# Graph network kernel, one core: a different order of ScalarE's copies and TensorE's matmuls at the turn from one batch of edges to the next

## What is computed

```
edge_index = jnp.stack([src, dst])
x = _layernorm(x + _L0_gnn_ref(x, src, dst), axis=-1)          # mean of the neighbours
x = _layernorm(x + _L1_gnn_ref(x, edge_weight, edge_attr_3, edge_index, w1, b1, w2, b2), axis=-1)
```

## Time and profile before

| | us |
|---|---|
| median of 3 runs | 3803.33 |
| lowest and highest | 3798.77, 3803.84 |
| the profiled execution | 3798.03 |
| its span, first to last instruction | 3796.3 |

### The profile page before, as it was taken

The page is one execution under the profiler, slowest core; times in us unless marked ns, Lnnn a source line. Parts: engine busy times, 40 slices in busy tenths (PEclk is TensorE's granted clock), DMA queues, the critical chain, the costliest instruction groups (busy, mean ns, idle before and its releaser), DMA issues.

```text
span 3796.3 us, 58108 instructions
## 1 busy us (share of the span) xinstructions
PE 3310.6 (87%) x17312; PEld 1902.1 (50%) x17312; DVE 2762.8 (73%) x3470; ACT 2061.5 (54%) x2391; POOL 2786.3 (73%) x2915
## 2 busy tenths in 40 slices
PE   4999999999999883399999999999999999999963
PEld 3898889898989783222323232333323232323232
DVE  5787877787878785467777777777777777777765
ACT  4777777776777660145454545454554545454520
POOL 6777777777777776677777777777777777777746
PEclk9999999999999995599999999999999999999975
DMA  4122222222122211122222222222222222222211
GB/s 100 39 57 41 52 43 43 50 44 54 40 55 43 50 48 29 39 57 53 62 55 59 55 59 55 59 58 56 62 52 62 55 59 54 59 55 59 57 28 26
DMA packets 188428, 197.65 MB, mean 52 GB/s; under 512 B 60241, under 2 KB 149427, under 8 KB 188085
## 3 DMA queue, kind: packets, MB, share of 16 engines
q1 hardware_dynamic: 95508, 149.13, 13.7%
q0 software_dynamic: 92832, 47.72, 9.7%
HBM read 134.02 MB, written 62.59 MB: 52 GB/s over the span
## 4 chain that ended last, share of the span: by engine, by line
PE 70%; ACT 12%; DVE 5%; POOL 5%; issue 5%; DMA 1%; SPq 0%; ACTq 0%; DVEq 0%; POOLq 0%
PE ps_r L940 19%; PE ps_r L990 17%; PE ps_m L1027 10%; PE ps_m L940 10%; PE ps_r L1018 8%; ACT prod_room L822 8%; POOL ngot L667 4%; DVE unit L1645 3%; PE ps_m L1037 2%; PE ps_r L1002 2%; ACT f_across L829 2%; PE ps_r L924 1%; ACT hot_s L739 1%; PE ps_m L1043 1%; ACT hot_s L742 1%
## 5 line engine op out<-in xcount | busy, mean ns | idle before, releaser
L688 POOL DMA_INDIRECT got<-x_d,idx x1564 | 1506.2, 963 | 530.6 <-issue 504.7
L822 ACT ACTIVATE prod_room<-ps_r,bias_col 128x1024 f32<-128x1024 f32 x392 | 435.9, 1112 | 780.0 <-PE ps_r L990 531.9
L940 PE MATMUL ps_r<-x_hi,hot_s 128*128 128x448 f32 x1974 | 741.6, 376 | 41.7 <-ACT hot_s L742 41.7
L1645 DVE TENSOR_TENSOR x_room<-radial_more,ps_r 128x1024 f32<-128x1024 f32 x392 | 475.0, 1212 | 384.0 <-PE ps_r L1018 252.3
L990 PE MATMUL ps_r<-hid,wc 64*128 64x512 f32 (+1 forms) x2352 | 669.8, 646 | 81.2 <-ACT prod_room L822 72.9
L940 PE MATMUL ps_r<-x_lo,hot_s 128*128 128x448 f32 x1974 | 733.0, 371 | 0.0
L739 ACT ACTIVATE hot_s<-rows,minus_row 128x512 fp32r<-128x512 f16 (+1 forms) x658 | 449.0, 764 | 244.0 <-PE ps_m L940 206.2
L1018 PE MATMUL ps_r<-ft,repeat 32*128 32x512 f32 (+1 forms) x2352 | 553.4, 639 | 1.1 <-ACT ft L848 0.6
L1645 DVE TENSOR_TENSOR unit<-prod_room,ps_r 128x1024 f32<-128x1024 f32 x392 | 451.1, 1213 | 106.9 <-PE ps_r L1018 102.0
L940 PEld LDWEIGHTS ps_r<-x_hi,hot_s 128*128 128x128 f32 x1974 | 378.3, 192 | 75.5 <-issue 43.0
L990 PEld LDWEIGHTS ps_r<-hid,wc 64*128 64x128 f32 x2352 | 178.8, 186 | 448.8 <-ACT prod_room L822 255.3
(11 more groups left out here) (203 smaller groups left out, 4438.4 us busy)
## 6 DMA issues: line engine op xcount, KB each, us to landing
hid<-weight_t SPq DMA_DIRECT2D x196, 256.0 KB
run_d<-runs_t SPq DMA_DIRECT2D x194, 256.0 KB
got<-x_d,idx POOLq DMA_INDIRECT x1564
rows<-code_d SPq DMA_DIRECT2D x47, 160.0 KB
frame_d<-x_sb SPq DMA_DIRECT2D x7, 1008.0 KB, 4.5
frame<-frame_d SPq DMA_DIRECT2D x98, 72.0 KB
frame_b<-frame_d SPq DMA_DIRECT2D x98, 72.0 KB
rows<-code_d SPq DMA_DIRECT2D x47, 128.0 KB
```

The source lines that it names most:

```text
L688: pool.indirect_dma_start(got[k][:, t, :], None, x1_d, bass.IndirectOffsetOnAxis(ap=idx[k][:, t:t + 1], axis=0)).then_inc(got2_landed[k], 16)
L822: act.activation(radial_s[u][:, :, 0:w], radial_slot[:, :, 0:w], ACT.Identity, bias=bias_col[:, c:c + 1]).then_inc(radial_copied, 1)
L940: mm = pe.matmul(found[BANK_OF[k][g]], hot_s[k][:, a, g, :], part[:, a * LN * D:(a + 1) * LN * D], start=(a == 0 and n == 0), stop=(a == B ...
L1645: dve.tensor_tensor(product[q][h][:, :, 0:w], radial_s[u][:, :, 0:w], spread_slot[(k + s_ + 1) % 2][:, :, 0:w], ALU.mult).then_inc(multipl ...
```

## The change

On ScalarE the copy of the summed values moves from the head of a batch's part to a place behind the copy of the scalar features and the copy of the last radial unit. On TensorE the first radial unit of the next batch moves from behind the features' transposes to a place ahead of the messages' transposes. Nothing is added or removed.

```diff
@@ ScalarE, layer1
-                    if not first:
-                        copy_summed(b - 1)
                     act.wait_ge(got2_landed[k], 16 * (T * i + n))
                     if not isinstance(b, int) or b > 1:
                         act.wait_ge(turned, b - 1)
                     act.copy(turned_in[k][:, 0:n, 0:MUL], got[k][:, 0:n, 0:MUL]).then_inc(f0_copied, 1)
                     copy_radial(b, UNITS - 1, w)
+                    if not first:
+                        copy_summed(b - 1)
                     act.copy(idx[k][:, :], src_all[:, bass.ds((b + 2) * T, T)]).then_inc(idx_ready, 1)
@@ TensorE, layer1
                     if not first:
                         sum_products(b - 1, 3)
+                    if not final:
+                        radial(b + 1, 1 - k, 0, later)
+                    if not first:
                         turn_messages(b - 1)
                     turn_features(b, k, w)
-                    if not final:
-                        radial(b + 1, 1 - k, 0, later)
                     spread_features(b, k, 0, w)
```

## The result

The changed kernel takes 3809.66 us in the median of 19 runs, the kernel before 3800.15 us in 19 runs: slower by 9.5 us, a ratio of medians of 1.0025. The ratio on record is 1.003, with a 95% interval from 1.0023 to 1.0037; it lies near the ratio of the means, which one changed run of 3826.70 us, at a mean granted clock of 0.918 against 0.948 in the others, pulls up. The forecast was slower by 21 us, 3825 with a range from 3814 to 3840, so the direction was right and the size was over twice too large.

What follows compares the result with a forecast made beforehand. The prediction took TensorE's chain, with ScalarE copies and a VectorE product between, as the bound. The spread moves from 5.20 to 5.42 us after unit 5; 97 turns x 0.22 = 21.3 us on 3803.3 gives 3825 us, range 3814 to 3840.

Steps and rivals of the forecast that it cites:

- Steps 1 and 2: TensorE's turn: unit 0 starts 2.42 us after unit 5, once that is copied, and takes 1.06 us, to R + 3.48.
- the new wait for `ft`: TensorE ahead of the spread: 0.75 us idle until ScalarE has copied `ft`, a copy that unit 0 hid before.
- what else moved: Later messages, earlier scalar copy and GpSimd release: claimed covered, costing nothing in steady state, at most a few us at the start.
- the signs that were named: Changed profile: waits ahead of unit 0 and spread, spread 5.4 to 5.5 us after unit 5, period 21.1 to 21.2 us.
- Step 3: TensorE's messages' transposes: the sums' copy stays hidden with 0.41 us of cover; transposes take 0.61 us, to R + 4.09.
- R: The start of radial unit 5 on TensorE, from which the times of a turn are counted.
- Step 4: Features' transposes: ScalarE's copy of `ft` starts 0.69 us after them, takes 0.59 us, ends at R + 5.37, nothing hiding it.
- The turns alternate between the two halves: Before the change, unit 5 to first spread is 5.16 us in one turn, 5.24 in the next; mean 5.20.
- no term below is a clock term: TensorE's message loop: granted clock is 1.00, its upper level of 2.4 GHz, so no forecast term depends on the clock.
- A gain from the filled gap: Rival: TensorE's gap ahead of the transposes shrinks and none opens behind; 51 us less, 3752 us; 7 in 100.
- The rival that GpSimd sets the period: GpSimd's gathers, not the turn, set the period, so 0.2 us on TensorE vanishes: no change, 3803 us; 6 in 100.
- The rival of dearer handovers: Several handovers cost more than their rows: 0.35 to 0.45 us a turn, 3837 to 3847 us; 9 in 100.

Runs made afterwards that it cites:

- the three runs with the early rotation: VectorE rotates next batch's features ahead of products 5 to 7: kernel before, 3797.72 us; changed kernel, 3810.71; kernel before with ScalarE's new order, 3789.66.
- the run that undoes it: Changed kernel with turn 0 alone in TensorE's old order, features' transposes ahead of radial unit 0: 3805.86 us, ratio 1.0016 to the kernel before.
- the last experiment: Kernel before with rotation made early, ScalarE's new order, and TensorE's features' transposes directly after the last sums, ahead of the messages': 3768.59 us, ratio 0.9912.
- TensorE's part alone: Kernel before with only TensorE's order new, ScalarE's copies in the old order: 4095.03 us in the median of two runs, ratio 1.0772.

## Why the prediction was right or wrong

- **Direction and mechanism: right, the size partly by luck.** The loop lost 5.2 us where 21.3 were forecast, a quarter; that the whole came to nearly half is due to turn 0, which was not in the sum. Steps 1 and 2 were measured as forecast (unit 0 at 2.42 us, the transposes at 3.48). The copy of the sums was hidden, the new wait for `ft` is there (0.67 us for a forecast 0.75), the handover from `ft` to the spread was 0.06 us, at the lower bound that was chosen, and what else moved was covered: from the spread to the next unit 5 it is 15.69 us before (2519.32 to 2535.01) and 15.70 after (2525.71 to 2541.41). Of the signs that were named, the waits came, but the spread stood at 5.24 us and not 5.4 to 5.5, the period at 20.94 and not 21.1 to 21.2, and VectorE's wait ahead of its first product at 0.56 and not 0.7, each by the same error.
- **Step 3 was mis-sized: this is the step that failed.** It took the distance from the messages' to the features' transposes, 0.61 us, as the time of the transposes. Their time is 0.49 us, as measured in the changed kernel and in the three runs with the early rotation that have the messages' transposes directly ahead of the features'. In the kernel before, the other 0.12 us were a wait for VectorE's rotated features, and the prediction had both ends at hand: ready at R+3.39, started at R+3.52, 0.13 us apart, much like the 0.12 us of handover in its own step 3. It checked that the features were ready before the new start and not whether they set the old one.
- **Step 4, the same error again.** The 0.69 us from the transposes to the copy of `ft` are 0.63 us where the transposes follow others without a wait (2524.44 to 2525.07); they last 0.60 instead of 0.65 us. With 0.49 and 0.63 the forecast's own sum is 2.42 + 1.06 + 0.49 + 0.63 + 0.58 + 0.06 = 5.24 us, which is what was measured, and 0.04 us a turn more than the 5.20 before.
- **"The turns alternate between the two halves": read, but not followed.** The alternation of 5.16 and 5.24 us was a sign of that hidden wait. VectorE starts its last rotation step later in one half, and the features' transposes follow it by 0.13 us, as in these rows of the kernel before:

```profile
2537.92 0.56 DVE L1666 TENSOR_TENSOR f_along<-part 128x384 f32<-128x384 f32 x1
```

```profile
2538.61 0.65 PE L1002 MATMUL ps_r<-ident,f_along 128*128 128x128 f32 x4
```

  In the changed kernel the alternation is gone from the turn.
- **Turn 0 was counted as one turn's 0.2 us.** It costs 3.1 us in the trace, and 3.3 to 3.8 us come back in the run that undoes it. The prediction had looked only at the turns inside the loop, and its "no term below is a clock term" holds there alone.
- **The sum as measured** is 5.2 us of loop and 3.1 of turn 0, 8.3 us. The two profiled executions lie 10.7 us apart: 0.8 us arose ahead of the first radial unit and 1.4 behind the last turning back, where nothing was changed, and 8.5 in between (2059.4 and 2067.9 us from the one to the other). Of the 9.5 us between the medians, 4.3 are left for turn 0, inside its 3.2 to 6.8 us; a closer division stays open.
- **The base.** 3803.3 us was the median of three runs. With 19 it is 3800.15, so 3.2 of the 15.3 us between 3825 and 3809.66 are the base's error and not the change's.
- **The rivals.** A gain from the filled gap did not appear: the gap ahead of the transposes did close, as the advice of the Trainium skill ("Perfetto Trace Analysis", Optimization Strategy) would have it, and opened again ahead of the spread. With work that depends on nothing in the turn, the same advice did pay: the last experiment fills the gap with the features' transposes and wins 31 us. The rival that GpSimd sets the period was wrong for this change, but it was nearer than the prediction had it. The 20.0 us a batch leave out the waits at batch heads and after each 112th gather; with them it is 20.56, as the last experiment shows. The rival of dearer handovers was wrong: they came out at the lower end.

## What to carry to other kernels

The distance between two instructions on one engine is a duration only if nothing released the second. Before a distance is used as a term, take each wait that the second one carries, add a handover to its releaser's end, and see whether the sum is the start in the row; a distance that alternates between two halves of a loop is a sign of such a release. Moving an instruction into a gap pays when what it had been covering does not need cover: here unit 0 had been hiding a copy by ScalarE, and the features' transposes, made independent of the turn, could fill the gap instead. The peeled first round has its own chain and its own clock, and has to be laid out apart.

## What the runs showed of the hardware

- **A gap of 2 us can cost the clock too.** With TensorE's part alone, an idle time of 1.9 to 2.0 us in each batch, behind a stretch at a granted clock of 1.00, was followed in every other batch by a stretch near the lower level of 1.2 GHz (4.6 us at 0.52 in the turn shown), and the loss was 294 us where the waits alone had been put at 160. The other batches have the same gap and keep their clock, so its length alone does not decide. The 0.67 and 0.30 us gaps of the changed kernel left the clock at 1.00. The Trainium skill, in "TensorE: Matmul & The Clock Gate", section "HAM oscillation — how this bites in real kernels", describes a loop whose waits are longer than its bursts of matmuls and which falls back to the lower clock each time round. This trace differs: the wait is short against the work (TensorE is busy 1730 of 2000 us), and still half of the batches fell back.
- **Four transposes of 128x128** take 0.49 us from the start of one set to the start of the next at a granted clock of 1.00, whether or not the first set came after a wait. The profile gives a set 0.60 us when it directly follows another set, and 0.65 or 0.66 when it follows a wait or matmuls of another shape.
- **GpSimd's indirect gathers** run at a pitch of 1.25 us, but after each 112th there is a longer stop in the traces: 2.8 to 3.0 us from one gather to the next where the gathers are the bound, 2.8 to 5.3 us in the kernel before. It comes by count and not by time: the stops are 112 gathers apart both where that is 144 us (the last experiment) and where it is some 167 us (TensorE's part alone, where GpSimd also waits for ScalarE's copy of the indices at other places). What it is the runs do not show.
